# Writing out a loop of chunk steps in a kernel of graph mixing, Mamba and LSTM

## The reference

```python
h = relu(adj @ layernorm(x) @ gcn_w + gcn_b)        # graph mixing
h = layernorm(h) * ln_g + ln_b
xz = h @ w_in; xc, z = xz[:, :256], xz[:, 256:]
u = silu(conv4(xc))
dbc = u @ w_xp; dt = softplus(dbc[:, :8] @ w_dt + b_dt)
B, C = dbc[:, 8:24], dbc[:, 24:]
hst = exp(dt * A) * hst + dt * B * u                # scan over 8192 tokens, 256 x 16 states
y = hst @ C + u * D_skip
x = x + (y * silu(z)) @ w_out
l = lstm(layernorm(x))                              # one sequence of 8192 steps, 128 units
x = x + 2 * l + prefix_sum_term(l) + suffix_sum_term(l)
```

## Time and profile before

| | |
|---|---|
| median of 3 runs | 1691.53 us (1689.65 to 1695.6) |
| the profiled execution | 1688.01 us, its span 1686.2 us |
| PE busy | 1551.6 us, 92% of the span |
| DVE busy | 1463.6 us, 87% |
| POOL, ACT busy | 1051.1 us (62%), 1002.9 us (59%) |
| chain that ended last | PE 38%, DVE 29%, issue 14%, ACT 3% |

### The profile page before, as it was taken

How to read it: one execution, slowest core, us unless ns; L and a number is a source line. 1 busy time by engine, 2 the same in 40 slices (tenths; PEclk the granted TensorE clock), 3 DMA queues, 4 the chain that set the end, 5 groups by cost and what they waited for, 6 DMA issues and landing times.

```text
span 1686.2 us, 21143 instructions
## 1 busy us (share of the span) xinstructions
PE 1551.6 (92%) x5282; PEld 797.4 (47%) x5282; DVE 1463.6 (87%) x1668; ACT 1002.9 (59%) x2093; POOL 1051.1 (62%) x490
## 2 busy tenths in 40 slices
PE   6999999999899989999999999999987678999994
PEld 2444434444344434343444444344432226999993
DVE  8406999999899999999999999899998995557998
ACT  2254666667575747575766666575757554555552
POOL 4024978787777869787878787878776851001221
PEclk9999999999999999999999999999998899999997
DMA  8977756666567666666667666666620202000002
GB/s 310 345 251 244 251 204 237 219 222 226 199 226 234 210 223 218 223 232 207 218 224 237 202 234 216 208 230 213 229 75 0 94 6 106 0 0 0 0 0 100
DMA packets 52073, 298.31 MB, mean 177 GB/s; under 512 B 5522, under 2 KB 5522, under 8 KB 19092
## 3 DMA queue, kind: packets, MB, share of 16 engines
q1 hardware_dynamic: 49680, 293.30, 50.9%
q10 hardware_dynamic: 2308, 4.20, 0.6%
HBM read 285.68 MB, written 11.80 MB: 176 GB/s over the span
## 4 chain that ended last, share of the span: by engine, by line
PE 38%; DVE 29%; issue 14%; ACT 3%; DVEq 2%; POOL 1%; ACTq 0%; POOLq 0%
PE bank L514 20%; DVE work L1118 15%; PE bank L441 7%; DVE work L1068 5%; PE bank L446 3%; PE bank L543 3%; PE bank L559 3%; DVE work L1141 2%; DVE work L1076 2%; PE bank L550 1%; PE bank L552 1%; DVE work L1172 1%; POOL work L918 1%; DVE work L1177 1%; PE bank L485 1%
## 5 line engine op out<-in xcount | busy, mean ns | idle before, releaser
L514 PE MATMUL bank<-ring,xh 128*128 128x512 f32 x2048 | 960.5, 595 | 14.9 <-DVE xh L1006 14.9
L1118 DVE TENSOR_TENSOR_SCAN work<-bank,hstate,work 128x512 f32<-128x512 f32 x512 | 627.5, 1266 | 16.4 <-ACT bank L768 11.1
L903 POOL TENSOR_TENSOR work<-work 128x1024 f32<-128x1024 f32 x210 | 501.8, 2390 | 212.0 <-DVE work L1076 204.0
L514 PEld LDWEIGHTS bank<-ring,xh 128*128 128x128 f32 x2048 | 390.6, 191 | 462.8 <-issue 436.4
L768 ACT ACTIVATE bank<-work,a_neg 128x512 f32<-128x512 f32 x512 | 344.9, 686 | 305.9 <-DVE work L1118 304.3
L1068 DVE TENSOR_TENSOR work<-work,bank 128x1024 f32<-128x1024 f32 x256 | 309.7, 1215 | 39.7 <-issue 16.2
L1076 DVE TENSOR_TENSOR work<-work,bank 128x1024 f32<-128x1024 f32 x182 | 216.2, 1194 | 0.0
L446 PE MATMUL bank<-bc_parts,sel 96*128 96x512 bf16 x512 | 193.9, 388 | 23.4 <-DVE work L1068 17.8
L441 PE MATMUL bank<-work,w_sb 128*128 128x512 f32 (+2 forms) x352 | 181.2, 611 | 36.5 <-ACT work L758 19.1
L968 POOL TENSOR_TENSOR work<-work 128x256 f32 x32 | 28.5, 892 | 237.5 <-ACT work L807 237.5
L863 POOL TENSOR_TENSOR work<-work 128x1024 f32<-128x1024 f32 x48 | 113.6, 2367 | 80.5 <-ACT work L665 80.3
(11 more groups left out here) (144 smaller groups left out, 1582.1 us busy)
## 6 DMA issues: line engine op xcount, KB each, us to landing
ring<-adj_t SPq DMA_DIRECT2D x256, 1024.0 KB, 4.8
xh<-x_rows SPq DMA_DIRECT2D x16, 256.0 KB, 6.4
work<-x_t SPq DMA_DIRECT2D x16, 256.0 KB, 4.7
x_scratch<-work ACTq DMA_DIRECT2D x16, 256.0 KB, 5.2
work<-x_scratch SPq DMA_DIRECT2D x1, 4096.0 KB, 14.0
out_t<-work SPq DMA_DIRECT2D x16, 256.0 KB, 2.8
xl_scratch<-work SPq DMA_DIRECT2D x13, 256.0 KB, 5.3
ring<-xl_scratch SPq DMA_DIRECT2D x1, 3328.0 KB, 12.9
```

The source lines that it names most:

```text
L514: last = nc.tensor.matmul(mixed[:, :], xn[:, j, :], a, start=(j == 0), stop=(j == BLK - 1))
L903: nc.gpsimd.tensor_tensor(out=acc, in0=hc[0] if n == 1 else acc, in1=hc[n % 2], op=ALU.add).then_inc(y_added, 1)
L1118: nc.vector.tensor_tensor_scan(hb[s % 2][:, h, :], da[h], dbu[s % 2][:, h, :], hstate[:, HV * s + h:HV * s + h + 1], ALU.mult, ALU.add).th ...
```

## The change

The loop disappears. `iterations` calls `step` 19 times with an integer k, on all five engines, and its argument `eng` goes, so lines below it move up by five (line 1118 of before is line 1113 of after, 1068 is 1063, 1076 is 1071, 758 is 753, 768 is 763).

```diff
-        def iterations(eng, step):
+        def iterations(step):
 
 
             def flags(k):
                 return k < NC, 1 <= k <= NC, 2 <= k <= NC + 1, 3 <= k <= NC + 2
-            for k in range(4):
-                step(k, k % 2, *flags(k))
-            with eng.Fori(4, NC - 1, 2) as k:
-                step(k, 0, True, True, True, True)
-                step(k + 1, 1, True, True, True, True)
-            for k in range(NC, NC + 3):
+            for k in range(NC + 3):
                 step(k, k % 2, *flags(k))
...
-            iterations(sp, step)
+            iterations(step)
...
-            iterations(dve, step)
+            iterations(step)
```

## The result

The written-out kernel takes 1672.43 us (median of 4 runs, 1671.33 to 1673.12) and the kernel before 1692.11 us (4 runs, 1689.65 to 1695.6). The ratio is 0.9882, with a 95% interval of 0.9863 to 0.9900: the change is a gain of 19.7 us. Run once more beside later experiments it took 1670.93 us against 1691.27, a ratio of 0.9880 (0.9865 to 0.9895). The forecast was 1673.5. Of all executions in this document one, of the kernel in which PE, POOL and SP loop, ran at a lower granted clock (1699.68 us); its ratio leaves that one out.

What follows compares the result with a forecast made beforehand. DVE was taken as the engine to look at, stalled at five jumps back: 1688.01 - 16.5 - 1.6 = 1669.9 us for an execution like the profiled one, median predicted 1673.5 us; 8 in 10 range 1664 to 1682.

Steps and rivals of the forecast that it cites:

- The bound and the stall: DVE in the loop: long steps hold no more work but a 3.3 us stall, its late first instruction after each jump.
- The stalls' 16.5 us: Five jumps back on DVE: each loses its stall of 3.29 us, a gain of 16.5 us.
- ACT's jump at 0: ACT's 4.07 us of issue at each jump lies beside DVE's own stall, so removing it gains 0.
- The register term: DVE's register arithmetic in the loop: 0.13 us a step over 12 steps, 1.6 us gained; bounds 0 and 3.6.
- The longer stream at 0: Fetching the instructions of steps 4 to 15 once each, more for PE: hidden, cost 0; about 33 packets on q8.
- rival C: PE's instruction fetches show, 3.8 us a step over twelve steps, and the kernel slows to 1718 us; chance 0.03.
- Rival A: The jump costs only itself: DVE's branches give 0.4 us, registers 1.6 at most; time about 1690 us; chance 0.05.
- the figure cited: The Trainium skill's some 108 ns for a compare-and-branch, which the prediction said agrees with DVE's recorded branch of 0.07 us.
- Rival B: Straight code on DVE and ACT stalls now and then: three 2.92 us stalls in twelve steps, about 1682; chance 0.05.
- Before and after the loop at 0, with 2 us either way: Steps 0 to 3, 16 to 18 and the LSTM keep their instructions: 0, with 2 us either way for memory layout.
- the 78.1 that the prediction named as a sign: The gain is right if all steps from 3 to 15 are 78.1 us long at DVE's first product.
- Rival D: PE and DVE's coupling loosens, so at most half of DVE's 16.2 us output-projection wait goes, 8 us: 1665; chance 0.03.

Runs made afterwards that it cites:

- the two counts of jumps: Kernel before, loop kept on all engines with a longer body: six steps, one jump back, 1678.53 us; four steps, two jumps, 1681.96 us.
- another move: Written-out kernel with PE's output projection moved to the start of slot 11, before the adjacency piece: 1642.92 us, ratio to before 0.9708.
- the last two kernels: Written-out kernel with PE's output projection moved earlier, 1642.92 us; written-out kernel with DVE's scalar_tensor_tensor swapped before the output projection's read-out in slot 12, 1648.34 us.

## Why the prediction was right, point by point

**The bound and the stall.** Right. DVE's own missing instruction was the cause of the long steps: with DVE looping alone they are there, and with the length of POOL's body the same kind of stall can be switched on. The stalls' 16.5 us came back whole: 18.09 in the loop, less 1.4 for the short steps, is 16.7.

**ACT's jump at 0.** Right for the change as made: with ACT written out and DVE looping, the long steps are as much over the plain ones as before, 3.2 us on average against 3.3. The side remark, "If only DVE's jump went ... ACT would still be in time", is right for the exponentials, but the loop was 3.6 us longer, nearly all in two steps in which PE's clock fell after waiting for ACT.

**The register term.** Its size was right, its place wrong. I took 1.6 us "on DVE" and said of PE, POOL and SP "All this is 0". The short steps did become 78.12 us from 78.24, 12 x 0.12 = 1.4 us. But POOL's registers alone make a step 0.22 us longer, by the scalar_tensor_tensor behind POOL's product; PE's cost nothing. DVE's own cost nothing either: with DVE looping alone the plain steps took 78.01 us, less than written out; DVE came to the scalar_tensor_tensor later behind POOL's product there, and it was shorter (2648 ns on average). In the kernel before the two partly cancel. How the 0.12 divides exactly isn't settled, and that 1.4 us came out close to the 1.6 taken is in part luck.

**The longer stream at 0.** Right: PE looping or not makes 0.1 us of difference over the twelve steps. q8 carried 29 packets, where I had worked out 33, and q14 40 in place of 71. This refutes rival C by experiment. Rival A falls with the two counts of jumps and with DVE alone. Where it says that the recorded branch agrees with the figure cited, the size is right and no more: the row is 0.07 us, a third shorter. Rival B did not occur: no step from 4 to 15 is over 78.12 us.

**Before and after the loop at 0, with 2 us either way.** Too tight for one execution: outside the loop the two profiled ones differ by 2.49 us, with 0.84 more in step 3, 3.28 more in step 16 and 1.63 less behind it. Step 3 was 78.94 us, not the 78.1 that the prediction named as a sign. The time from the end of the loop on changed by 1.65 us, inside its 2. The sum for an execution like the profiled one, 1669.9, was therefore 2.8 us under the 1672.69 of the one that was profiled; the median was 1.1 us under the 1673.5 of the forecast, and that it was so close is partly luck, since the medians' difference is 1.6 us more than the 18.1 summed.

**Rival D.** Wrong as a part of this change (L1029 still waits 15.0 us), but what it pointed at was there to be had by another move, and more of it than I gave.

## What to carry to other kernels

A loop's jump back can cost microseconds on an engine whose body is long: look for a wait of "issue" whose count is the number of jumps, on the engine that sets the pace, and compare the length of a step with a jump to one without. Such a stall costs only what that engine has not queued, and a jump on another engine may be free, or, like ACT's here, show only through the clock of an engine that it makes idle. Once steps are even, compare the duration of the same instruction in different places: one that is twice as long as elsewhere may wait inside for something that no wait row names.

## What the runs showed of the hardware

*Bodies and jumps.* From the branch to the first instruction of the body, by the executed instructions that the records show in the body:

| engine | without a stall | with one |
|---|---|---|
| POOL | 153, 249 and 303: 0.25 to 0.29 us | 453 and 473: 2.49 to 2.89 us |
| SP | 141 and 279: 0.27 to 0.33 us | 415: 5.47 us |
| ACT | | 303, 603 and 903: 4.39 to 4.76 us |
| DVE | | 384: 4.59 to 5.01 us; 765: 4.90 and 5.59; 1146: 6.02 |
| PE (without the matmuls) | 498: 0.27 to 0.28 us | 994 and 1491: 4.55 to 4.66 us |

On POOL, SP and PE the longer bodies stall and the shorter ones don't. The limit isn't one count for all: 303 on POOL go without a stall and 303 on ACT do not, and why isn't shown.

*DVE and POOL exclude each other.* A DVE scalar_tensor_tensor with both inputs in SBUF and a POOL tensor_tensor don't run at the same time: whichever comes second gets next to nothing done until the first ends (1.08 of DVE's 1.22 us and 2.23 of POOL's 2.36 come after it). DVE's takes 1.22 us where POOL is idle. Behind a POOL product it takes what is left of that product and 1.08 us more: in steps 4 to 15 that is 1.45 to 1.48 us in the last two kernels and 2.62 to 3.07 in the others. A POOL product behind it takes 3.23 us in place of 2.36. The Trainium skill ("SBUF — State Buffer", SBUF: two separate sides) says that the two share a port pair under an exclusive lock, held for the whole instruction, also against a DVE operation with two SBUF inputs. The trace agrees, with the ends 1.08 to 1.10 us apart in each of 15 steps of all fourteen profiles. DVE's products with one input in PSUM keep their 1.2 us beside POOL.
